# Dummy matmuls in TensorE's waits ahead of the first state step, and other orders on all engines, in a fused attention, adapter and recurrence kernel

## What is computed

```
y   = x @ W_subject.T + b_subject                 # a weight chosen by item (8 of them)
q,k,v = y @ Wq.T, y @ Wk.T, y @ Wv.T (+ biases)   # 16 heads of width 16
s   = sum over 5 freqs of alpha * sin(2 pi sim / freq + phi)      # sim = q k / scale
w   = sigmoid(s); w = w / (sum(w) + 1e-10)
x1  = x + layernorm((w v) @ Wo.T + bo) * gamma + beta
z   = layernorm(x1 + relu(x1 @ W1_lang + b1) @ W2_lang + b2) * gamma_lang + beta_lang
c   = sigmoid(f) * c + sigmoid(i) * tanh(g)       # 32 steps over the items; f, i, g from z_t and c
out = x1 + tanh(z @ Wo'.T + c_final @ Uo'.T + bo')
```

## Time and profile before

| what | value |
|---|---|
| median of 3 runs | 341.5 us (341.22, 341.5, 343.73) |
| profiled execution | 340.6 us, its span 338.8 us |
| mean granted clock of TensorE in it | 0.948 |
| busy: VectorE (DVE) | 286.6 us, 85% of the span |
| busy: TensorE (PE) | 277.5 us, 82% |
| busy: ScalarE (ACT) | 270.2 us, 80% |
| busy: GpSimd (POOL) | 56.0 us, 17% |

### The profile page before, as it was taken

How to read it: one execution, slowest core, us unless ns; L and a number is a source line. 1 busy time by engine, 2 the same in 40 slices (tenths; PEclk the granted TensorE clock), 3 DMA queues, 4 the chain that set the end, 5 groups by cost and what they waited for, 6 DMA issues and landing times.

```text
span 338.8 us, 7109 instructions
## 1 busy us (share of the span) xinstructions
PE 277.5 (82%) x2532; PEld 164.0 (48%) x2532; DVE 286.6 (85%) x617; ACT 270.2 (80%) x405; POOL 56.0 (17%) x58
## 2 busy tenths in 40 slices
PE   5846768466869889998988988989898998999890
PEld 5735337343437754545455544545663454433350
DVE  2179995998987999999999998999999999454356
ACT  1299698989998999999999999999999974323123
POOL 5000000222020002234400316033013321210000
PEclk9999796758797999999999999999999999999997
DMA  5688046592033455416514320651144161010006
GB/s 168 205 268 321 1 67 178 111 263 55 0 57 102 71 157 159 70 41 119 110 21 99 103 33 1 142 102 17 18 127 86 32 134 25 3 31 0 2 17 231
DMA packets 32229, 31.74 MB, mean 94 GB/s; under 512 B 10690, under 2 KB 24130, under 8 KB 32194
## 3 DMA queue, kind: packets, MB, share of 16 engines
q1 hardware_dynamic: 27266, 26.46, 29.3%
q0 software_dynamic: 4352, 4.20, 8.1%
q10 hardware_dynamic: 576, 0.64, 0.7%
HBM read 23.15 MB, written 2.10 MB: 75 GB/s over the span
## 4 chain that ended last, share of the span: by engine, by line
ACT 42%; DVE 27%; PE 14%; issue 11%; DMA 3%; POOL 2%; SPq 1%; DVEq 0%; ACTq 0%; POOLq 0%
ACT ang L1102 13%; ACT ang L1111 11%; DVE sc L1619 8%; PE pg L674 4%; ACT sc L1093 3%; DVE ang L1604 2%; ACT gat L1157 2%; DVE fc L1761 2%; PE pf L584 2%; ACT sc L1122 2%; PE pf L504 2%; DVE ang L1595 2%; PE pr L626 2%; ACT L1108 2%; ACT L1115 2%
## 5 line engine op out<-in xcount | busy, mean ns | idle before, releaser
L1619 DVE SCALAR_TENSOR_TENSOR sc<-ang,small,sc 128x512 f32<-128x512 f32 (+1 forms) x160 | 98.3, 637 | 1.3
L1111 ACT ACTIVATE ang<-ang,qs 128x2560 f32<-128x2560 int32 x32 | 77.0, 2427 | 1.5 <-DVE ang L1604 1.4
L1102 ACT ACTIVATE ang<-sc,phase 128x512 int32<-128x512 f32 (+1 forms) x126 | 72.3, 644 | 0.0
L674 PE MATMUL pg<-gate_u,cT 128*64 128x384 f32 x256 | 48.0, 496 | 5.0 <-DVE cT L1770 5.0
L665 PE MATMUL pg<-gate_w,zT 128*64 128x384 f32 x256 | 50.1, 498 | 0.8 <-DVE zT L1751 0.7
L1604 DVE TENSOR_SCALAR ang<-ang 128x2560 int32<-128x2560 int32 x32 | 47.2, 1484 | 0.9 <-ACT ang L1102 0.8
L1157 ACT ACTIVATE gat<-pg 128x384 f32<-128x384 f32 x32 | 15.5, 485 | 26.8 <-PE pg L674 26.8
L1595 DVE TENSOR_SCALAR ang<-sc,phase 128x256 int32<-128x256 f32 (+1 forms) x74 | 28.1, 417 | 5.2 <-ACT sc L1093 5.1
L584 PE MATMUL pf<-qm,kT 64*64 64x128 f32 x512 | 19.8, 298 | 11.3 <-DMA qm<-qT 3.3
L674 PEld LDWEIGHTS pg<-gate_u,cT 128*64 128x64 f32 x256 | 16.1, 136 | 26.2 <-issue 16.0
L665 PEld LDWEIGHTS pg<-gate_w,zT 128*64 128x64 f32 x256 | 15.5, 136 | 19.6 <-issue 14.7
(11 more groups left out here) (111 smaller groups left out, 464.4 us busy)
## 6 DMA issues: line engine op xcount, KB each, us to landing
wc<-in_cond SPq DMA_DIRECT2D x30, 257.0 KB, 3.6
w<-in_up SPq DMA_DIRECT2D x32, 128.2 KB, 2.7
wa<-in_down SPq DMA_DIRECT2D x32, 66.0 KB, 2.2
xt<-in_xt SPq DMA_DIRECT2D x8, 256.0 KB, 3.9
xt<-rows POOLq DMA_DIRECT2D x8, 256.0 KB, 4.9
w<-x POOLq DMA_DIRECT2D x8, 256.0 KB, 4.0
xg<-in_x SPq DMA_DIRECT2D x3, 512.0 KB, 4.8
qm<-qT SPq DMA_DIRECT2D x48, 32.0 KB, 2.1
```

Of the source, the lines that this page charges most:

```text
L674: mm = pe.matmul(pg[n % 2][u * L:(u + 1) * L, 0:GCOLS], cT[:, kc, :], gate_u[:, kc, u, :], start=False, stop=(kc == KC - 1), skip_group_ch ...
L1102: op = act.activation(ang[:, n % SLOTS, f, r], unit(n)[:, r], ACT.Identity, scale=TURN / FREQS[f], bias=phase[:, p * NF + f:p * NF + f + 1])
L1111: act.activation(a.bitcast(F32), a, ACT.Sin, scale=2 * PI_LOW / TURN, bias=qs[:, 3:4]).then_inc(sine_ready, 1)
L1619: op = dve.scalar_tensor_tensor(out=unit(n)[:, r], in0=sine, scalar=amp, in1=unit(n)[:, r], op0=ALU.mult, op1=ALU.add)
```

## The change

The list of every engine is put in another order, and TensorE's gets more dummy matmuls. In the program the new calls are 69: the block of 3 ahead of the first queries becomes one of 5, and 13 blocks of 2 to 9 are added (5, 5, 5, 5, 9, 4, 5, 7, 5, 2, 6, 3 and 6), the last one ahead of `output_part(0, 0)`. That makes 17 blocks in all. Two helpers, `shifted_wait` and `added_wait`, choose which semaphore to wait for; since `ADDED_BY_DMA` is empty, they wait for what was waited for before, and the new function `residual_added` on GpSimd is not called. No other instruction is added or taken away.

```
+ADDED_BY_DMA = ()
...
+        def added_wait(eng, q):
+
+            if q in ADDED_BY_DMA:
+                eng.wait_ge(x1_moved[q % 2], 16 * count(ADDED_BY_DMA, q))
+            else:
+                eng.wait_ge(x1_ready, sum(k not in ADDED_BY_DMA for k in range(q + 1)))
...
             spread_q(1, 0)
+            load_rest(0, 0)
+            load_cond(2, 1)
+            load_rest(0, 1)
+            load_rest(0, 2)
+            load_x(2)
+            load_rest(0, 3)
+            spread_q(1, 1)
...
             turn_tokens(0)
-            for _ in range(3):
+            for _ in range(5):
                 pe.matmul(pct[:, :], eye[:, :], eye[:, :], start=True, stop=True)
             queries(0, 0)
...
             queries(1, 1)
             keys(1, 1)
+            for _ in range(9):
+                pe.matmul(pct[:, :], eye[:, :], eye[:, :], start=True, stop=True)
+            scores(2)
+            for _ in range(4):
+                pe.matmul(pct[:, :], eye[:, :], eye[:, :], start=True, stop=True)
+            scores(3)
             weighted(0)
-            scores(2)
             weighted(1)
-            scores(3)
```

More of the change, by code:

```diff
@@ L767, in _ @@
             values(2, 0)
-            weighted(2)
+            values(2, 1)
             weighted(3)
-            values(2, 1)
+            for _ in range(7):
+                pe.matmul(pct[:, :], eye[:, :], eye[:, :], start=True, stop=True)
+            turned(0)
+            for _ in range(5):
+                pe.matmul(pct[:, :], eye[:, :], eye[:, :], start=True, stop=True)
             scores(4)
-            turned(0)
+            output_projection(0, 0)
             scores(5)
-            output_projection(0, 0)
             output_projection(0, 1)
@@ L788, in _ @@
             turn_normed(0)
+            for _ in range(6):
+                pe.matmul(pct[:, :], eye[:, :], eye[:, :], start=True, stop=True)
             output_part(0, 0)
+            output_part(0, 1)
             weighted(4)
             weighted(5)
-            output_part(0, 1)
             scores(6)
@@ L1264, in _ @@
             angle(9, 1)
+            sines(7, False)
+            tokens(3)
+            tokens(4)
+            residual_turned(0)
             angle(9, 2)
@@ L1361, in _ @@
             sines(18, False)
+            queries(3, 1)
             keys(3, 1)
@@ L1475, in _ @@
             squares(6)
+            sines(30, False)
             gates(19)
@@ L1683, in residual_added @@
                 dve.wait_ge(x1_part, q + 1)
-                if q in SHIFT_BY_DMA:
-                    dve.wait_ge(xt_shifted[q % 2], 16 * count(SHIFT_BY_DMA, q))
-                else:
-                    dve.wait_ge(xt_ready, sum(k not in SHIFT_BY_DMA for k in range(q + 1)))
+                shifted_wait(dve, q)
                 dve.tensor_tensor(x1[:, part(q)], x1[:, part(q)], xt[:, q % 2], ALU.add).then_inc(x1_ready, 1)
@@ L2030, in _ @@
+            shifted_language(2)
+            cell_step(7, 0)
+            divided(9, 0)
+            cell_step(7, 1)
             wrap(20)
-            cell_step(7, 0)
-            cell_step(7, 1)
-            divided(9, 0)
-            modulated(2)
+            angle(22, 0)
+            angle(22, 1)
             divided(9, 1)
-            shifted_language(2)
-            angle(21, 0)
             divided(9, 2)
+            state_copy(7)
             values(3)
-            state_copy(7)
+            wrap(21)
```

767 lines of the change are left out of this document (389 added, 378 removed).

## The result

| | before | changed |
|---|---|---|
| median of 12 runs each | 343.44 us (339.78 to 346.60) | 339.97 us (338.28 to 341.29) |
| ratio | 1 | 0.9912, 95% interval [0.9888, 0.9937] |
| profiled execution, its span | 340.6, 338.8 us | 338.96, 337.2 us |
| mean granted clock in it | 0.948 | 0.967 |

The kernel became faster by 0.9%, where 1.0% was forecast. (The ratio is worked out from the single runs; the quotient of the two medians is 0.990.) That agreement is better than the reasons for it, as will be seen: the two profiled executions differ by 1.6 us only, the medians by 3.5, and the sum of the prediction, 3.3 us, was made for the profiled execution of the kernel before. The time forecast, 338.2 us, is 1.8 us under the median measured.

The account below looks back on a forecast made before the run. VectorE, full up to 283 us except from 35 to 110 us, was taken as the bound, its idle time coming off the end; 1.1 + 3.1 - 0.9 = 3.3 us took 341.5 to 338.2 us, range 335.0 to 342.5.

Parts of the forecast that it names:

- The clock at 37 us: Group 1's first queries: clock holds, they take 1.73 us less, gain 1.1 us at `wrap(5)`; rival that it falls, 0.23.
- The dummies' price: Each dummy 0.28 us at full clock; the block of 5 ahead of the first queries delays everything behind by 0.36 us.
- The three waits that new work fills: VectorE's waits ahead of `residual(0)` (0.93 us), `modulated(0)` (0.75) and `divided(3, 0)` (1.42) go: 3.1 us gained.
- the second spread: SyncE's DMAs for group 1's queries end at 63.6 instead of 62.02 us; cost nothing, 0.5 us at worst.
- The normalising: GpSimd's pair: wait gone ahead of `normalise(2)`, new ones of 0.9 us ahead of `normalise(0)` and `normalise(3)`; net loss 0.9 us.
- The end: Last stage: `normalise(7)` waits about 1 us for GpSimd and `output_part(7, 0)` goes last; both cost nothing, the tail keeps its length.
- The sum: Gains of 1.1 and 3.1 us less 0.9 make 3.3 us off the profiled execution.
- From the profile to the median: Profiled execution goes from 340.6 to 337.3 us; the runs' median stands 0.9 above it, so 341.5 becomes 338.2 us.
- The slower rival: Dummies from 45 us run at low clock and hold work up, 3.7 us slower than before, 345.2 us; chance 0.10.
- The clock's whole penalty: Low clock from 35 to 110 us: the skill's sum gives back 15 us, time 326 us; given next to no chance.

Follow-up runs that it names:

- The filled kernel: Changed kernel with more dummies in TensorE's waits at 61 to 64 and 78 to 84 us; ratio 0.9838 to the kernel before.
- The orders alone: Changed kernel with all new dummies taken out, every engine in the new order; ratio 1.0038 to the kernel before, median 343.81 us.
- the early blocks: Kernel before plus 22 dummies: 5 instead of 3 ahead of the first queries, four blocks of 5 up to group 1's transposes; ratio 0.9887.
- a block twice as long: Kernel before with new dummies only, its block ahead of group 1's first scores 18 calls instead of 9; ratio 0.9866, against 0.9873 with 9.
- the best kernel: Changed kernel with group 1's second spread earlier, waits at 61 to 84 us filled, 8 dummies ahead of group 1's first queries; 0.9813, 338.18 us.

## Why the prediction was right, and where it was not

The ratio (0.990 forecast, 0.991 measured) and the direction hold, and by the experiments the agreement is partly luck. The sum was twice what the profiled execution shows (3.3 us against 1.7), and the median of the kernel before was 1.9 us over the one that the forecast started from; the two errors have opposite signs in the ratio. Step by step:

- *The clock at 37 us.* Right in the profile: 1.98 us instead of 3.61. With the start of the division at 50.50 instead of my 51.97 and `wrap(5)` ended by 58.27, the gain there, by the same comparison, is 58.27 - 0.78 = 57.5 against 60.10, 2.6 us where the sum had 1.1. The earlier start is 0.3 of it.
- *The dummies' price.* 0.28 us each, taken from a block of three whose duration includes the last one's end, was too high: from start to start the block of 5 took 1.11 us, 0.22 each. Of the 0.36 us of delay 0.09 came: the first queries began 0.84 us behind VectorE's first `yT` instead of 0.75 (at 12.94 us, as that `yT` was 0.28 us earlier).
- *The three waits that new work fills*, 3.1 us: gone, as said. But four new ones, 4.2 us, came. This is the step that failed. For the second spread I had the third scores at 65.2 (they began at 64.08) and took "nothing, and 0.5 us at worst", since "no call of VectorE waits for them soon". But `angle(8, 0)` waits for the copies of the fourth scores as well. VectorE had come to it at 74.03 with the first copy just done, and 4 us that it gains ahead of this place can't be kept if the scores don't gain them too. They gained 2.2, for they ran at the low clock behind waits of 3.07 and 1.75 us. The filled kernel shows it: with dummies there the wait of 2.17 us is gone.
- *The normalising.* The row with 0.88 us was put to the wrong part: it is `normalise(3)`, not `normalise(2)`. That wait is still there (0.92 us at 205.54), as the wrap stands still ahead of it, so it is neither gained nor lost. The new one ahead of `normalise(0)` did not come: VectorE waited 0.60 us for ScalarE ahead of the wrap, and GpSimd, whose second instruction then took 1.73 us and ended with the wrap, was done at 95.56, just as VectorE got there. Net 0 instead of -0.9. The Trainium skill tells of a pair of ports that the two engines share under a lock, which whichever starts first holds for its whole instruction (SBUF — State Buffer, SBUF: two separate sides). That GpSimd's instruction, 0.74 us long with VectorE idle, ended with the wrap fits this. That it began 0.20 us ahead of the wrap, and 0.46 us in the earlier trace rows, does not, and no run here settles it.
- *The end.* As long as before; right.
- *The sum* for the profiled pair: 2.6 + 3.1 - 4.2 = 1.5 against 1.66 measured at the last sigmoid. The prediction had 3.3.
- *From the profile to the median.* I added 0.9 us to both and so took the gain as the same in every execution. It isn't. The kernel before has a median of 343.4 over 12 and more runs; the three shown had 341.5. The changed one spreads half as wide. The orders alone are worth nothing (1.0038) and the early blocks most of it (0.9887), for they prevent a fall of the clock that my profile did not contain.
- *That the three filled waits "are won for the most part by order, and would stay won"* holds for the waits, which the orders alone remove too, and fails for the time: that kernel waits 4.6 us ahead of its first division and 2.3 us for ScalarE's angles, and gains nothing.
- *The slower rival*, dummies that hold work up: a block twice as long at full clock showed no cost in the runs and 0.4 us in the profiles. At the low clock it was not tried.
- *The clock's whole penalty.* The sum from the Trainium skill (TensorE: Matmul & The Clock Gate, Terms) gave an estimate of 15 us. The runs don't bear it out: with the clock at 0.98 from 35 to 110 us the best kernel gained 1.9%, 6.4 us, and the changed one 0.9% with 0.91.

Left open: how often the clock falls at each place, which fourteen profiles tell only roughly, why the first conditions are slow in some executions, and which of the new orders cost what.

## What to carry to other kernels

Look at more than one profile of a program whose TensorE idles often: the clock falls in different waits in different executions, and a sum made on one of them prices only its own falls. Dummy matmuls in TensorE's waits are a cheap insurance; one block of twice the length did no harm that the runs show. When an engine gets to a place earlier, ask whether what it needs there gets earlier as well, and price the calls behind a wait of TensorE at the low clock too. And don't take idle time of a nearly full engine as won one to one: of 2.0 us more of waiting 0.4 us reached the end of the stage, and 1.4 us put to use came back as other waits.

## What was unexpected of the hardware

The same program and the same time of start: the first values took 1.97 us in one execution and 3.23 in another (granted clock 0.83 from 20 to 30 us), after the same instructions at the same times within 0.02 us up to the scores at 22.15. And the first conditions took 3.4 to 3.6 us in four of the fourteen profiles (634 ns for one matmul at the median) and 1.95 us in the others (379 ns), though they began at 8.6 to 9.1 us in all. In three of the four the granted clock reads 1.00 meanwhile, in the filled kernel 0.50.
